# The second edge list's chunks stored in the order they are dealt, and put in place by gathers in the mean stage

## The reference, cut to what matters

```python
h = relu(layernorm(x)); x = x + L0(h)   # mean over edges of h[src], summed by dst
h = relu(layernorm(x)); x = x + L1(h)   # two weighted sums of h[src] by dst, weights by edge type
h = relu(layernorm(x)); x = x + L2(h)   # attention: softmax over edges, summed by src, v and k of dst
h = relu(layernorm(x)); x = x + L3(h)   # sum over edges of h[dst], summed by src
```

## Time and profile before

| | us |
|---|---|
| median of 3 runs | 12145.7 (12131.9 to 12184.8) |
| span of the profiled execution, first to last instruction | 10339.8 |
| median minus span | 1805.9 |
| POOL busy | 7070.6 (68% of the span) |
| DVE busy | 6562.4 (63%) |
| PE busy | 6181.9 (60%) |
| ACT busy | 2732.1 (26%) |

### The profile page before, as it was taken

The page is one execution under the profiler, slowest core; times in us unless marked ns, Lnnn a source line. Parts: engine busy times, 40 slices in busy tenths (PEclk is TensorE's granted clock), DMA queues, the critical chain, the costliest instruction groups (busy, mean ns, idle before and its releaser), DMA issues. The chain is left out here.

```text
span 10339.8 us, 113558 instructions
## 1 busy us (share of the span) xinstructions
PE 6181.9 (60%) x29757; PEld 4616.2 (45%) x29757; DVE 6562.4 (63%) x14941; ACT 2732.1 (26%) x8897; POOL 7070.6 (68%) x7382
## 2 busy tenths in 40 slices
PE   8844577777777746565655656666666434444443
PEld 2223355555555544444444445555555333333333
DVE  7799877777777746666666656666666733333333
ACT  0033211111111114444444425555555400000000
POOL 0056677777777737777777667777777577777776
PEclk6555688888898867777777789999999855555555
DMA  2000132322323233333333334444444422222224
GB/s 89 0 22 11 34 74 72 74 72 72 74 72 74 70 46 56 55 55 55 55 55 55 45 89 112 112 111 111 112 111 111 79 56 54 54 54 54 54 54 59
DMA packets 1357093, 691.02 MB, mean 67 GB/s; under 512 B 1166772, under 2 KB 1207448, under 8 KB 1355688
## 3 DMA queue, kind: packets, MB, share of 16 engines
q0 software_dynamic: 267936, 604.23, 22.4%
q1 hardware_dynamic: 1088520, 79.52, 7.9%
HBM read 579.32 MB, written 103.90 MB: 66 GB/s over the span
## 5 line engine op out<-in xcount | busy, mean ns | idle before, releaser
L1621 POOL DMA_INDIRECT l_kv<-kv_tab,l_words x1616 | 1575.9, 975 | 504.7 <-issue 467.0
L865 POOL DMA_INDIRECT l_rows<-h_tab,l_index x1616 | 1539.1, 952 | 506.6 <-issue 444.4
L1217 POOL DMA_INDIRECT l_rows<-h_tab,l_index x1616 | 1531.5, 948 | 507.5 <-issue 458.4
L557 POOL DMA_INDIRECT l_rows<-h_tab,l_words x1616 | 1524.7, 943 | 515.9 <-issue 411.4
L600 PE MATMUL l_sums<-l_onehot,l_rows 128*128 128x128 f32 x3232 | 826.6, 438 | 1294.9 <-issue 1112.8
L1352 PE MATMUL l_sums<-l_weighted,l_rows 128*128 128x256 f32 x3232 | 1172.6, 527 | 661.9 <-issue 568.0
L600 PEld LDWEIGHTS l_sums<-l_onehot,l_rows 128*128 128x128 f32 x3232 | 719.6, 328 | 1401.9 <-issue 1295.4
L588 DVE TENSOR_TENSOR acc<-acc,l_sums 128x128 f32 x1616 | 464.4, 287 | 1324.1 <-PE l_sums L600 1118.9
L1231 ACT ACTIVATE l_weighted<-l_onehot,l_weights 128x128 f32<-128x128 bf16 x3232 | 987.6, 388 | 1057.8 <-DVE l_onehot L508 1024.5
L1352 PEld LDWEIGHTS l_sums<-l_weighted,l_rows 128*128 128x128 f32 x3232 | 810.4, 263 | 828.9 <-issue 595.0
L1279 DVE TENSOR_TENSOR acc<-acc,l_sums 128x256 f32 x1616 | 678.8, 420 | 676.9 <-PE l_sums L1352 524.5
(11 more groups left out here) (318 smaller groups left out, 10935.4 us busy)
## 6 DMA issues: line engine op xcount, KB each, us to landing
l_rows<-h_tab,l_index POOLq DMA_INDIRECT x3232, 2.5
l_kv<-kv_tab,l_words POOLq DMA_INDIRECT x1616
l_rows<-h_tab,l_words POOLq DMA_INDIRECT x1616, 2.5
l_words<-dealt_src SPq DMA_DIRECT2D x404, 38.0 KB
dealt_src<-h SPq DMA_DIRECT2D x4, 3136.0 KB, 25.3
l_attr<-in_edge_attr SPq DMA_DIRECT2D x44, 272.0 KB, 4.5
h_tab<-h SPq DMA_DIRECT2D x21, 448.0 KB, 3.0
kv_tab<-acc SPq DMA_DIRECT2D x7, 896.0 KB, 4.0
```

The source lines that it names most:

```text
L557: pool.indirect_dma_start(rows[b][:, j, :], None, table, bass.IndirectOffsetOnAxis(ap=words[k % 3][:, at + j, 0:1], axis=0)).then_inc(rows ...
L865: pool.indirect_dma_start(rows[b][:, j, 0:D], None, table, bass.IndirectOffsetOnAxis(ap=index[q // Q16 % WORDS][:, q % Q16 * H + j, :], ax ...
L1217: pool.indirect_dma_start(rows[b][:, j, :], None, h_tab, bass.IndirectOffsetOnAxis(ap=index[q // Q16 % WORDS][:, q % Q16 * H + j, :], axis ...
L1621: pool.indirect_dma_start(kv[s][:, e, :], None, kv_tab, bass.IndirectOffsetOnAxis(ap=words[s][:, e, 0:1], axis=0)).then_inc(kv_ready[b], 16)
```

## The change: what it does

- In the sort, turn 1 makes no `shift`. `find_chunks` makes tables `ends`, `rises` and `owner` instead, from which the place of each chunk can be found. POOL makes two tables more (`stages`, `chunk_no`). The second list is no longer filled with zeros; one block of 128 zero rows is.
- `Dealer` no longer makes `begun`, `beyond`, `closed` or row numbers. The first deal keeps all of it in a subclass, `Scatterer`.
- In the first deal, `Chunks` finds for every chunk of the second list its row in `staged`: 13 times four matmuls on PE and a copy on ACT, and 104 instructions on DVE with an accumulated output, of 392 columns each.
- In the list stage, SP stores the 128 chunks of deal g to rows 128 g and on of `staged`, a plain DMA. POOL has only the gathers. The loads of the edge words stand at other places in SP's program: the first four ahead, then block k + 3 at the third group of block k.
- In the mean stage, POOL issues 104 gathers of up to 128 chunks from `staged`, six buffers deep, and SP stores them in the list `by_src`, between the seven stores of `h_tab`.

The diff, cut to what the text speaks of:

```diff
@@ rank_phase, sync
-                for at in range(0, ZS, NB * D):
-                    n = min(NB * D, ZS - at)
-                    sp.dma_start(src_flat[:, at:at + n], zero[:, 0:n]).then_inc(zeroed, 16)
+                sp.dma_start(staged[NOWHERE:, :], zero[:, 0:ZS]).then_inc(zeroed, 16)
@@ rank_phase, vector
+                def in_parts(of, parts):
+                    ch.link(nc.vector.tensor_scalar(high[:], of[:], 6, 6, ALU.logical_shift_right, ALU.logical_shift_left))
+                    ch.link(nc.vector.tensor_copy(parts[0][:], high[:]))
+                    ch.link(nc.vector.tensor_scalar(high[:], of[:], LOW - 1, None, ALU.bitwise_and))
+                    ch.link(nc.vector.tensor_copy(parts[1][:], high[:]))
+
+                def find_chunks():
+                    nc.vector.scalar_tensor_tensor(line[:, 0:DEALS], stages[:, 0:DEALS], tcol[:, 2:3], back[:], ALU.subtract, ALU.add)
+                    ch.link(nc.vector.memset(line[:, DEALS:], float(NOWHERE + LIFT)))
+                    nc.vector.tensor_copy(rise[:, 0:1], line[:, 0:1])
+                    ch.link(nc.vector.tensor_tensor(rise[:, 1:], line[:, 1:], line[:, 0:DEALS], ALU.subtract))
+                    in_parts(rise, rises)
+                    ch.link(nc.vector.tensor_scalar(line[:], whole[:], tcol[:, 2:3], None, ALU.add))
+                    nc.vector.tensor_copy(rise[:, 0:DEALS], line[:, 0:DEALS])
+                    ch.link(nc.vector.tensor_tensor(rise[:, DEALS:], line[:, DEALS:], tcol[:, 3:4], ALU.add))
+                    in_parts(rise, ends)
+                    ch.link(nc.vector.tensor_scalar(beyond[:], tcol[:, 1:2], tcol[:, 0:1], rest[:, 0:1], ALU.add, ALU.add))
+                    ch.link(nc.vector.scalar_tensor_tensor(owner[:], tile_no[:], beyond[:, 0:1], reached[:], ALU.is_lt, ALU.mult))
@@ Dealer
-        nc.vector.tensor_tensor(self.beyond[:, 0:n, :], iota, of(self.opened, lo), ALU.is_ge).then_inc(self.parted, 1)
-        nc.vector.tensor_tensor(self.begun[:, 0:n, :], iota, of(self.first, lo), ALU.is_ge).then_inc(self.parted, 1)
...
-        nc.vector.tensor_tensor(self.closed[b][:, 0:n, :], self.begun[:, 0:n, :], self.beyond[:, 0:n, :], ALU.subtract).then_inc(self.framed, 1)
...
-        for part in range(2):
-            nc.tensor.matmul(self.sums[b][:, size:size + 1], self.closed[k][:, i, :], self.shift[part][:, g:g + 1],
-                             start=(part == 0), stop=(part == 1))
+        self.tensor_rows(pe, g)
...
+    def scalar_out(self, act, g, out, dealt):
+        self.nc.scalar.activation(out, dealt, ACT.Copy).then_inc(self.copied, 1)
+
+    def store(self, sp, g):
+        r = g % RING
+        sp.wait_ge(self.copied, g + 1)
+        sp.dma_start(self.table[g * P:(g + 1) * P, :], self.out[r].bitcast(I32).rearrange("p k w -> p (k w)")).then_inc(self.sent[r], 16)
@@ Chunks (new)
+    def tensor(self, pe, m):
+        nc, b, n = self.nc, m % 2, span_tiles(m)
+        own = self.owner[:, m * P:m * P + n]
+        if m >= 2:
+            pe.wait_ge(self.counted, (m - 1) * CT)
+        for part in range(2):
+            nc.tensor.matmul(self.ends_of[b][0:n, 0:DEALS + 1], own, self.ends[part][:], start=(part == 0), stop=(part == 1))
+        for part in range(2):
+            last = nc.tensor.matmul(self.rises_of[b][0:n, 0:DEALS + 1], own, self.rises[part][:], start=(part == 0), stop=(part == 1))
+        last.then_inc(self.looked, 1)
...
+    def vector(self, dve, k):
+        m = k // CT
+        n = span_tiles(m)
+        if k % CT == 0:
+            dve.wait_ge(self.taken, m + 1)
+        if k:
+            dve.wait_ge(self.counted, k)
+        self.nc.vector.scalar_tensor_tensor(self.passed[0:n, :], self.ends_of[m % 2][0:n, 0:DEALS + 1], self.chunk_no[0:n, k:k + 1],
+                                            self.risen[m % 2][0:n, :], ALU.is_le, ALU.mult,
+                                            accum_out=self.total[0:n, k:k + 1]).then_inc(self.counted, 1)
@@ deal_phase, vector
+                    if k >= 2:
+                        chunks.vector(dve, k - 2)
@@ sum_deal_phase
+                for k in range(WORDS):
+                    load(k)
+                attributes(0)
                 for q in range(QUADS):
...
+                    if q % Q16 == 2 and WORDS <= q // Q16 + WORDS - 1 < TILES // T16:
+                        load(q // Q16 + WORDS - 1)
                     if q % ATTR == 8 and q // ATTR + 1 < DEALS // ATTR:
                         attributes(q // ATTR + 1)
+                    if q < DEALS:
+                        deal.store(sp, q)
...
-                    if LAG <= q < DEALS + LAG:
-                        deal.gpsimd(pool, q - LAG)
-                deal.gpsimd_end(pool)
@@ mean_phase
+                for k in range(CHUNKS):
+                    sp.wait_ge(fetch_ready[k % FETCH], 16 * (k // FETCH + 1))
+                    m, n = k // CT, span_tiles(k // CT)
+                    sp.dma_start(lists[k % CT, m * P:m * P + n], fetched[k % FETCH][0:n]).then_inc(fetch_stored[k % FETCH], 16)
+                    r = k // SHARE - 1
+                    if k % SHARE == SHARE - 1 and r >= 0:
+                        sp.wait_ge(h_ready, r + 1)
+                        sp.dma_start(rows[r], h[:, part_of(r), :]).then_inc(h_stored, 16)
...
+                for k in range(CHUNKS):
+                    if k >= FETCH:
+                        pool.wait_ge(fetch_stored[k % FETCH], 16 * (k // FETCH))
+                    n = span_tiles(k // CT)
+                    pool.indirect_dma_start(fetched[k % FETCH][0:n], None, staged, bass.IndirectOffsetOnAxis(ap=chunk_row[0:n, k:k + 1], axis=0)
+                                            ).then_inc(fetch_ready[k % FETCH], 16)
```

More of the change, by code:

```diff
@@ L257, in rank_phase @@
         lists = sb("lists", [BINS, DEALS + 1])
+        stages = sb("stages", [BINS, DEALS + 1])
+        rest = sb("rest", [BINS, 1])
+        beyond = sb("beyond", [BINS, 1])
+        line, rise = sb("line", [BINS, DEALS + 1]), sb("rise", [BINS, DEALS + 1], I32)
+        high = sb("high", [BINS, DEALS + 1], I32)
         reached = sb("reached", [BINS, TILES], BF16)
@@ L642, in __init__ @@
         frame = lambda name: sb(name, [BINS, GB, P], BF16)
-        self.begun, self.beyond = frame("begun"), frame("beyond")
-        self.closed, self.left, self.next = ([frame(f"{name}{b}") for b in range(2)] for name in ("closed", "left", "next"))
-        self.rows = sb("rows", [P, RING], I32)
+        self.left, self.next = ([frame(f"{name}{b}") for b in range(2)] for name in ("left", "next"))
         ps = lambda name: own.enter_context(nc.psum_tensor(f"{tag}_{name}", [P, 512], F32))
@@ L730, in tensor, with tensor_rows @@
         last.then_inc(self.grouped, 1)
+    def tensor_rows(self, pe, g):
+        pass
     def scalar(self, act, g):
@@ L751, in gpsimd @@
         pool.nop(nofuse=True)
-        out = self.out[r].bitcast(I32) if self.ints else self.out[r]
         pool.indirect_dma_start(self.table, bass.IndirectOffsetOnAxis(ap=self.rows[:, r:r + 1], axis=0),
-                                out.rearrange("p k w -> p (k w)"), None).then_inc(self.sent[r], 16)
-    def gpsimd_end(self, pool):
-        for r in range(RING):
-            pool.wait_ge(self.sent[r], 16 * (-(-(DEALS - r) // RING)))
-def deal_phase(nc, ranks, words, place, trash, table, sent, done_with):
+                                self.out[r].rearrange("p k w -> p (k w)"), None).then_inc(self.sent[r], 16)
@@ L764, in deal_phase @@
+def deal_phase(nc, ranks, shift, words, place, trash, table, sent, done_with, ends, rises, owner, chunk_no, chunk_row):
     with ExitStack() as own:
-        deal = Dealer(nc, own, "dst", ranks, WD, BF16, GB, place, trash, table, sent)
+        deal = Scatterer(nc, own, "dst", ranks, shift, WD, BF16, GB, place, trash, table, sent)
+        chunks = Chunks(nc, own, ends, rises, owner, chunk_no, chunk_row)
+        BLOCKS = -(-DEALS // GB)
         with nc.Block() as block:
```

209 lines of the change are left out of this document (157 added, 52 removed).

## The result

The changed kernel takes 11684.5 us (median of four runs, 11673.0 to 11703.0) against 12149.5 us for the kernel before (four runs, 12131.9 to 12184.8): ratio 0.9616, 95% interval 0.9598 to 0.9634, 465 us less. The forecast was 11738 us, 408 us less, and the low end of its range, 11690, lies 5.5 us above the measured time.

The account below looks back on a forecast made before the run. POOL's issue rate was taken to bound the list stage. The terms 6 + 52 - 514 + 48 = -408 us, from the median of 12145.7, gave 11738 us, range 11690 to 11880, with chance 0.77 for the forecast.

Parts of the forecast that it names:

- sort: Sort stage: about 16 DVE steps in place of five to find the chunks, +6 us, ends 4 and 9.
- first deal: First deal: 104 added scans on DVE, 96 of them in the loop where DVE is the bound, +52 us, ends 45 and 75.
- list stage: List stage: 391 scatters leave POOL, the period per group falls from 6.324 to 5.01 us, -514 us.
- mean stage: Mean stage: 104 new POOL gathers set its length, +43 us plus 5 for stalls, +48; ends 36 and 90.
- the scan's price: First deal: one 392-column scan on DVE lasts 560 ns by its width, taken as 0.54 us after a little overlap.
- rival 2: Mean stage bound by transfers, not by POOL's issue: 1.7 us a turn, 11780 us in all; chance 0.07.
- rule on two SBUF operands: Mean stage: seven DVE divisions with both operands in SBUF could each hold a gather back 1.55 us, 11 us in all.
- time outside the span: Whole kernel: the 1805.9 us between profiled span and median time was taken to lie outside the span and carried over unchanged.
- rival 1: List stage paced by DVE and PE: saving 354 to 450 us instead of 514, 11800 to 11900 us; chance 0.11.
- Rival 3: PE's granted clock falls and PE bounds the list stage, slower than before, 12535 us; decisive at mean clock 0.61; chance 0.02.
- rival 4: List stage period set by the rows' transfers, not POOL's issue: only 106 us are added, 12252 us; chance 0.02.
- The sign that I had set for rival 1: List stage: first to last gather in 2100 to 2180 us, POOL waiting for the sums of four groups back.

Follow-up runs that it names:

- before: The kernel before, unchanged; the trace the prediction read has a span of 10339.8 us, its timed median is 12149.5 us.
- after_ref: The changed kernel, unchanged, timed in a later job of the short kind: 9952.5 us against 10358.2, ratio 0.9606.
- before_again: The kernel before, unchanged, profiled once more, in the long kind: 12293.3 us.
- after_again: The changed kernel, unchanged, profiled on the same chip right behind the repeat of the kernel before, long kind: 11836.1 us.
- pool_stores: The changed kernel with the second list's 391 stores given back to POOL as indirect DMAs, row numbers counted up beforehand: 10456.7 us, short kind.
- pe_rows: The changed kernel with the list stage's 782 small matmuls and 391 activations put back, SyncE still storing: 9934.7 us, short kind.
- after: The changed kernel, unchanged, in its first profiled execution, of the long kind: 11678.05 us.
- two_edits_2: The changed kernel with 782 small matmuls and 391 activations back and the h_tab stores on ACT's queue: 11723.5 us against 12161.4, long kind.

## Why the prediction was right or wrong

Its terms, beside two pairs of like executions: the trace of before with after_ref (short), before_again with after_again (long, one job). First-to-last and stage-to-stage times from the rows of indirect DMAs, in us.

| step | predicted | short | long |
|---|---|---|---|
| sort | +6 | +5.4 | +5.5 |
| first deal | +52 | +52.2 | +49.3 |
| list stage | -514 | -514.0 | -598.5 |
| mean stage | +48 | +55.3 | +91.6 |
| relation stage | 0 | +0.8 | +0.8 |
| the rest | 0 | +12.7 | -6.0 |
| span | -408 | -387.6 | -457.3 |

The last row is the difference of the spans: 9952.2 - 10339.8 and 11834.3 - 12291.6. The short column sets two jobs side by side, and before's trace is 4 to 20 us shorter than its later runs in the short kind, so the +12.7 of the rest needn't be a cost of the change; within one job the medians differ by 406, where the prediction has 408.

- **Sort and first deal** are right, in size and cause, the scan's price partly by luck: it lasts 608 ns where I read 560 off two widths, and overlaps with the next step by 65 ns where I allowed 20. The two errors cancel, 0.54 us for 0.543.
- **List stage**, in the kind of execution that I read: right to the microsecond, and for the reason given. pool_stores brings 513 us of it back, pe_rows changes nothing, the granted clock is 0.97 (I had asked for 0.86 or more), and POOL has no waits but its gaps, so DVE at 4.6 of 5.01 us a group didn't pace it. The term was mis-sized for the long kind: it measured 598.5. There each of before's 1616 + 391 indirect DMAs cost 3050.1/2007 = 1.52 us of the stage, and each of after's 1616 cost 2451.6/1616 = 1.52; 391 x 1.52 = 594. By POOL's own account in before_again a scatter took 0.99 us and 1.59 of idling, most of it for ACT's copy, which stood behind PE:

```profile
L865 POOL DMA_INDIRECT l_rows<-h_tab,l_index x1616 | 1544.7, 956 | 512.3 <-issue 484.0 <-DVE l_index L883 14.4 <-remote 6.2
...
L753 POOL DMA_INDIRECT dealt_src<-tmp,src_rows x391 | 386.4, 988 | 622.1 <-ACT src_rows L746 527.3 <-issue 94.8
```

```profile
L1042 POOL DMA_INDIRECT l_rows<-h_tab,l_index x1616 | 1528.9, 946 | 938.1 <-issue 450.6 <-remote 246.0 <-PE l_sums L1117 226.1
```

  The last row is of after_again: with the scatters 1008.5 us of POOL's time went, and 425.8 came back as waits of the gathers.
- **Mean stage.** In the short kind 104 gathers in 140.9 us, 1.37 us apart on the mean, and +55 for +48: right within its ends, with 19 us of waits for stores (after_ref), so rival 2 had a grain of truth. The stalls at 5 us were too few. In the long kind +92, just past the upper end of 90: PE is held while POOL gathers, h comes late, SyncE waits for it and the ring with it. Rival 2 would have given the same number for another reason.
- The Trainium skill's rule on two SBUF operands (the page "SBUF — State Buffer", section "Who interferes with whom") would have added 11 us; the same section also says that a tensor_tensor step of DVE wasn't seen to stall a DMA. By the traces it does, and by little: in after the only two gathers over 1.05 us (1599 and 1464 ns for 946) each overlap a division, in after_ref four of the seven divisions hold a gather, up to 1980 ns. That is 0.8 us in all in after and 3.2 in after_ref, too small to count.
- **The step that failed** is the one on the time outside the span: "I carry that difference over unchanged, since nothing in the change has a row there". The difference of 1805.9 us wasn't outside the span at all; the span of every other run here is 1.7 to 1.8 us short of its time. It was inside, in the gather stages, where indirect DMAs cost more, and the change takes 391 - 104 = 287 of them away. Of the miss, -457 for -408, the list stage makes -84.5, the mean stage +43.6, first deal and sort -3 and the rest -5. A difference of 15% between a span and the times beside it should have been a rival of its own: that the trace is of another kind of execution, and the sum scales with what differs. Why the long kind exists stays open.
- **Rivals 1, 3 and 4** didn't come. The sign that I had set for rival 1, waits of POOL for sums of four groups back, did appear in the long kind (226 us, and 246 remote), but with POOL as the cause and not DVE's or PE's load: the relation stage, where both have less to do, shows the same waits. The mean clock of after's list stage is 0.86 in the long kind too, as in the earlier trace rows. (Rival 3's equation gives x = 0.21, not 0.22; the mean clock of 0.61 stands.)

## What to carry to other kernels

Compare the span of a trace with the times it is to explain before anything is read from it; here they agreed within 1.8 us whenever the trace was of the run that was timed, and where they lay 1806 us apart it was of another kind of execution, which a stage that the change leaves alone showed. Count indirect DMAs as a resource of the whole core: in the gather stages here each cost 1.25 to 1.31 us in one kind of execution and 1.43 to 1.73 in the other, so this kernel gained by issuing 287 fewer of them, and where PE works beside them their price depends on the kind. And a wait that looks like a fault (SyncE behind h) may be what lets another engine through: take it away on the chip before calling it a loss.

## What the runs showed of the hardware that was not expected

- The same program runs in two kinds of executions, 10350 and 12130 to 12320 us, per job and not per chip. They differ where POOL issues indirect DMAs back to back and another engine waits for PE: the sort (558.4 and 558.6 us in before) and the first deal, with scatters 1.6 us apart (637.2 and 632.7), take nearly the same time in both.
- In the long kind PE falls to one matmul in 2.8 us, or its increments come up to nine microseconds late in the relation stage (in two_edits_2 ACT's copy of a block of PE's transposes starts 31 us after them), and in bursts. It ends after POOL's last gather: 2.4 us after it in the relation stage, some 5 to 8 behind the 49 gathers of L1429, 10.9 in two_edits_2. The gathers' own duration (944 ns) doesn't change. In the relation stage POOL's standstill adds up to some 0.95 us for four gathers, as one pause for each four or one wait for each sixteen.
- In the relation stage of after only about 600 of 808 increments of PE's count of summed pairs are in the record, in after_ref about 800. What holds PE is open. Attention loses most in the long kind (721 us), and why is open. The Trainium skill, on the page "NOTIFIC — the notification-queue block", section "Overflow: three behaviours, one of which stalls the engine", says that a full notification queue can be set to stall the engine that writes to it. A stalled PE would fit that, the missing records would not, since a queue set that way drops none by the page. No run here shows it, since each run shown was recorded; whether an unrecorded one is of either kind wasn't tried.
- Empty instructions on POOL, 10 ahead of each group in the relation stage and 40 in layer 3, cost no time in the short kind: 2021.4 and 2016.0 us.
